# Queries ahead of scores in six slots, the first norm step behind the outputs, statistics in other slots, one value copy ahead, and one matmul for both parts of the reciprocals

## What is computed

```python
lat, ctx = layer_norm(layernorm(x)), layer_norm(context)
q = lat @ Wq;  k, v = split(ctx @ Wkv);  k = apply_rope(k, cos, sin)
attn = softmax(clip(q @ k.T * 64**-0.5, -11, 11))        # per batch and head
x = x + (attn @ v) @ Wo + bo                             # first layer
h = rmsnorm(layernorm(x)) * gamma1
q2 = h @ Wq + bq;  k2, v2 = split((h @ Wdown + bdown) @ Wup + bup)
att = softmax(q2 . k2 over the 8 of a group / sqrt(8))   # 16 x 16 per token
x1 = layernorm(x) + (att . v2) @ Wo + bo
h2 = rmsnorm(x1) * gamma2;  gate = softmax(h2 @ Wg + bg)
out = x + x1 + sum_e gate[e] * (h2 @ We[e])
```

## Time and profile before

| | us |
|---|---|
| median of 3 runs | 317.58 |
| the three runs | 317.51, 317.58, 318.62 |
| the profiled execution | 318.85 |
| its span (first to last instruction) | 317.0 |
| granted TensorE clock, mean | 0.996 |

### The profile page before, as it was taken

How to read it: one execution, slowest core, us unless ns; L and a number is a source line. 1 busy time by engine, 2 the same in 40 slices (tenths; PEclk the granted TensorE clock), 3 DMA queues, 4 the chain that set the end, 5 groups by cost and what they waited for, 6 DMA issues and landing times.

```text
span 317.0 us, 6676 instructions
## 1 busy us (share of the span) xinstructions
PE 295.0 (93%) x2514; PEld 206.9 (65%) x2514; DVE 241.6 (76%) x448; ACT 164.0 (52%) x326; POOL 208.6 (66%) x207
## 2 busy tenths in 40 slices
PE   6888999999999999998999999999999999899983
PEld 6776576666668766665777676566786665486651
DVE  2985997675884849899888788977647699687856
ACT  2446456667443735573425555874426468404741
POOL 5445875765572839786645777498927588868764
PEclk9999999999999999999999999999999999999998
DMA  7563412111210111111111112011101100000001
GB/s 207 169 160 90 134 44 68 52 35 46 58 26 9 38 31 35 36 33 33 35 35 33 28 27 50 13 40 37 32 19 33 47 7 2 0 19 0 3 0 33
DMA packets 16319, 14.24 MB, mean 45 GB/s; under 512 B 4832, under 2 KB 11808, under 8 KB 16288
## 3 DMA queue, kind: packets, MB, share of 16 engines
q1 hardware_dynamic: 14992, 13.49, 16.2%
q10 hardware_dynamic: 1296, 0.33, 0.5%
HBM read 4.89 MB, written 0.52 MB: 17 GB/s over the span
## 4 chain that ended last, share of the span: by engine, by line
PE 54%; DVE 20%; issue 7%; POOL 5%; ACT 5%; DMA 4%; SPq 3%; POOLq 0%; ACTq 0%; DVEq 0%
PE pv L631 12%; PE sc L617 10%; PE sums L652 7%; PE side L738 4%; PE pj_k L555 3%; SPq L522 3%; DVE ks L1262 3%; PE side L814 2%; PE pj_k L557 2%; PE pj_k L556 2%; DMA kswap<-ksin 2%; DMA sin_in<-in_L_xattn_sin_dram 2%; DVE ksin L1326 2%; ACT e L926 2%; POOL e L1768 1%
## 5 line engine op out<-in xcount | busy, mean ns | idle before, releaser
L1768 POOL TENSOR_SCALAR e<-e 128x1024 f32<-128x1024 f32 x64 | 71.6, 1118 | 64.2 <-ACT e L926 56.8
L926 ACT ACTIVATE e<-sc 128x1024 f32<-128x1024 f32 x64 | 65.6, 1025 | 31.3 <-PE sc L617 31.2
L617 PEld LDWEIGHTS sc<-qs,ks 64*128 64x128 f32 x768 | 49.6, 185 | 25.9 <-issue 24.0
L617 PE MATMUL sc<-qs,ks 64*128 64x256 f32 x768 | 62.5, 294 | 2.3 <-ACT e L926 2.2
L631 PE MATMUL pv<-e,v 128*64 128x256 f32 x512 | 62.3, 385 | 1.6 <-POOL e L1768 1.1
L1761 POOL TENSOR_TENSOR krot<-kcos,kswap 128x512 f32<-128x512 f32 x32 | 45.7, 1429 | 9.4 <-DMA kswap<-ksin 7.6
L631 PEld LDWEIGHTS pv<-e,v 128*64 128x64 f32 x512 | 34.1, 136 | 24.0 <-issue 6.8
L934 ACT ACTIVATE u<-pv 128x256 f32<-128x256 f32 x32 | 12.4, 386 | 61.6 <-PE pv L631 61.6
L1262 DVE TENSOR_TENSOR ks<-krot,ks 128x512 fp32r<-128x512 f32 x32 | 32.4, 1012 | 0.1
L1326 DVE TENSOR_TENSOR ksin<-pj_k,sinT 128x512 f32<-128x512 f32 x32 | 21.9, 685 | 3.8 <-PE pj_k L557 3.5
L918 ACT ACTIVATE v<-pj_k 128x512 f32<-128x512 f32 x28 | 16.5, 600 | 13.9 <-PE pj_k L557 13.5
(11 more groups left out here) (293 smaller groups left out, 578.1 us busy)
## 6 DMA issues: line engine op xcount, KB each, us to landing
kswap<-ksin SPq DMA_DIRECT2D x126, 64.0 KB, 2.0
ctx_in<-in_ctx_dram SPq DMA_DIRECT2D x4, 256.0 KB, 3.5
prod<-in_L_xattn_Wkv_dram SPq DMA_DIRECT2D x2, 512.0 KB, 6.3
x_in<-in_x_dram SPq DMA_DIRECT2D x1, 512.0 KB, 6.4
prod<-in_L_xattn_Wq_dram SPq DMA_DIRECT2D x1, 512.0 KB, 7.2
wo<-in_L_xattn_Wo_dram SPq DMA_DIRECT2D x1, 512.0 KB, 4.4
fwe<-in_L_ffn_We_dram SPq DMA_DIRECT2D x1, 512.0 KB, 4.4
out_dram<-x_in SPq DMA_DIRECT2D x3, 128.0 KB, 1.8
```

The source lines that it names most:

```text
L617: last = nc.tensor.matmul(sc[:, h, c * NT:(c + 1) * NT], ks[rows, j % 3, k_part, chunk], qs[rows, j % 2, q_part, :], start=(k_part + q_par ...
L926: nc.scalar.activation(e[:, j % 3, :, 2 * half:2 * half + 2, :].rearrange("p h c n -> p h (c n)"), sc[:, :, :], ACT.Exp, scale=SCALE).then ...
L1768: nc.gpsimd.tensor_scalar(a, a, EXP_HIGH, EXP_LOW, ALU.min, ALU.max).then_inc(s_clip, 1)
```

## The change

In slots where nothing stands on TensorE between the second half of the scores and the next keys but these keys (`queries_ahead`: 6, 9, 14, 17, 22, 25), the queries of the next pair are made ahead of `scores(slot, 0)`. Where the "a" step of a slot is `norm0` (`after_outputs`: 9, 17, 25), it stands behind `times_values` on TensorE, and its take behind `key_lo` on VectorE. `recS[:, 1]` becomes odd * rounded - rec: in even rows this is minus the reciprocal, rounded, in odd rows minus the rest. `spread` has -1 in an even and in the odd row next to it, so that one matmul adds both parts. It needs a second `affine_select` on GpSimd at the start and a small reduction in slot 0 for `odd`. The statistics of batches 2 and 3 go from slots 9 and 17 to slots 4 and 12 (batch 1 stays in slot 1). In slots 22 and 23 the first of two value copies goes ahead of the moe step.

```diff
--- before.py
+++ after.py
@@ -205,6 +205,18 @@
     return n < 4
 
 
+def queries_ahead(slot):
+
+    return 1 <= slot <= NPAIR - KEYS_AHEAD - 1 and not (side_step(slot - 1, "b") or side_step(slot - 1, "c")
+                                                       or value_units(slot - 1))
+
+
+def after_outputs(slot):
+
+    step = side_step(slot, "a")
+    return step is not None and step[0] == "norm0"
+
+
 def projections():
 
     units = []
@@ -311,7 +323,9 @@
 
 
         e_added = moe.rearrange("p t e d -> p (t e d)").rearrange("p (j c h n) -> p j c h n", j=2, c=2, h=2)
+
         recS = sb("recS", [128, 2, NT], fp32r)
+        odd = sb("odd", [128, 1])
 
         f_stat = sb("f_stat", [128, TT, 6])
         f_mv = sb("f_mv", [128, TT, 2])
@@ -721,8 +735,7 @@
                     for i in range(2):
                         p = 2 * int(name[4]) + i
                         dst = side[:, i * NT:(i + 1) * NT]
-                        nc.tensor.matmul(dst, spread[:, p, :], recS[:, 0, :], start=True, stop=False)
-                        last = nc.tensor.matmul(dst, spread[:, p, :], recS[:, 1, :], start=False, stop=True)
+                        last = nc.tensor.matmul(dst, spread[:, p, :], recS[:, 1, :], start=True, stop=True)
                 elif name == "out_proj":
                     if b == 0:
                         pe.wait_ge(ld["wo"], 16)
@@ -839,6 +852,8 @@
                 elif slot + 1 < NPAIR:
                     queries(slot + 1)
                 side_at(slot - 1, "c")
+                if queries_ahead(slot):
+                    queries(slot + 1)
                 if slot == 0:
                     keep_busy(WARM_UP["scores"], pv_bank)
                 if 0 <= slot < NPAIR:
@@ -846,13 +861,16 @@
 
                 if slot == 0:
                     keys(KEYS_AHEAD)
-                side_at(slot, "a")
-                if 0 <= slot + 1 < NPAIR and slot + KEYS_AHEAD < NPAIR:
+                if not after_outputs(slot):
+                    side_at(slot, "a")
+                if 0 <= slot + 1 < NPAIR and slot + KEYS_AHEAD < NPAIR and not queries_ahead(slot):
                     queries(slot + 1)
                 if 2 <= slot <= NPAIR and slot % 2 == 0:
                     sums(slot - 1)
                 if 1 <= slot <= NPAIR:
                     times_values(slot - 1)
+                if after_outputs(slot):
+                    side_at(slot, "a")
                 if slot == 0:
                     values(0)
                     values(1)
@@ -1135,9 +1153,15 @@
                 if 0 <= slot < NPAIR:
                     exps(slot, 1)
 
+                units = value_units(slot)
+                step = side_step(slot, "b")
+                if step and step[0].startswith("moe"):
+                    for n in units[:1]:
+                        value_copy(n)
+                    units = units[1:]
                 if slot < NPAIR - 3:
                     side_taken(slot, "b")
-                for n in value_units(slot):
+                for n in units:
                     value_copy(n)
                 if 0 <= slot + KV_AHEAD < NPAIR:
                     key_hi(slot + KV_AHEAD)
@@ -1345,7 +1369,9 @@
                 nc.vector.reciprocal(rec, sum_bank[:, 0:NT]).then_inc(s_rec, 1)
                 dve.wait_ge(s_rec, b + 1)
                 own(nc.vector.tensor_copy(recS[:, 0, :], rec))
-                split_lo(recS[:, 1, :], rec, recS[:, 0, :]).then_inc(s_recS, 1)
+
+                nc.vector.scalar_tensor_tensor(recS[:, 1, :], f(recS[:, 0, :]), odd[:, :], rec,
+                                               ALU.mult, ALU.subtract).then_inc(s_recS, 1)
 
 
             def tokens(b):
@@ -1676,7 +1702,10 @@
                 if slot == 0:
                     dve.wait_ge(s_const, 3)
                     nc.vector.tensor_copy(spread[:, :, :], spread_f[:, :, :]).then_inc(s_spread, 1)
-                side_taken(slot, "a")
+                    own(nc.vector.tensor_reduce(odd[:, :], ident.rearrange("p (a two) -> p two a", two=2)[:, 1, :],
+                                                AX, ALU.add))
+                if not after_outputs(slot):
+                    side_taken(slot, "a")
                 second_layer(slot, "early")
                 if 1 <= slot + 1 < NPAIR:
                     query_lo(slot + 1)
@@ -1684,13 +1713,19 @@
                     split_latT(b + 1)
                 if 1 <= slot + 1 < NPAIR:
                     key_lo(slot + 1)
+                if after_outputs(slot):
+                    side_taken(slot, "a")
                 second_layer(slot, "mid")
                 second_layer(slot, "late")
                 side_taken(slot, "b")
                 if more:
-                    if p == 1:
-                        ctx_statistics(b + 1)
-                        tokens_statistics(b + 1)
+
+                    if slot == 1:
+                        ctx_statistics(1)
+                        tokens_statistics(1)
+                    if p == 4 and b + 2 < NB:
+                        ctx_statistics(b + 2)
+                        tokens_statistics(b + 2)
                     if p == 2:
                         ctx_normalise(b + 1)
                         tokens_normalise(b + 1)
@@ -1744,7 +1779,10 @@
             nc.gpsimd.memset(sum_rows[:, 24:32], 1.0).then_inc(s_const, 1)
             own(nc.gpsimd.memset(spread_f[:, :, :], 0.0))
             sp_v = spread_f[:, :, :].rearrange("k (i q) (h c) -> k i q h c", q=2, h=2)
-            nc.gpsimd.affine_select(out=sp_v, in_=sp_v, compare_op=ALU.not_equal, fill=1.0, base=0,
+
+            own(nc.gpsimd.affine_select(out=sp_v, in_=sp_v, compare_op=ALU.not_equal, fill=-1.0, base=0,
+                                        pattern=[[-8, PAIRS // 2], [-64, 2], [-32, 2], [0, DH]], channel_multiplier=1))
+            nc.gpsimd.affine_select(out=sp_v, in_=sp_v, compare_op=ALU.not_equal, fill=-1.0, base=-1,
                                     pattern=[[-8, PAIRS // 2], [-64, 2], [-32, 2], [0, DH]], channel_multiplier=1)\
                 .then_inc(s_const, 1)
             ctx_rstd(0)
```

## The result

The changed kernel takes 314.12 us (median of 4 runs, 312.95 to 314.33) beside 317.54 for the kernel before on the same chip; the ratio is 0.9859 (95% interval 0.983 to 0.9888). The forecast was 312.6 in 310.8 to 315.3: faster, and inside the range. Measured once more, the changed kernel gave 313.19 beside 317.84, 0.9856 (0.984 to 0.9872).

What follows compares the result with a forecast made beforehand. The prediction took TensorE's stream as the bound in the loop over slots. Its terms, 1.73 + 0.2 + 1.28 + 0.66 + 1.0 + 0.1 = 5.0, taken from the median 317.58 gave 312.6 us, range 310.8 to 315.3.

Steps and rivals of the forecast that it cites:

- Slots 9 and 10, 17 and 18: Norm steps: 1.73 won in slots 9 and 10; 0.2 over slots 12 to 17, then 1.28 as in slot 10.
- the queries' place: Between scores and outputs: queries made ahead of the scores free their old place, 0.54 a slot, nothing in slot 6.
- Slots 12 to 16: Moved statistics make VectorE 1.66 late at first; some 1.1 is given back, 0.55 late at values(18) and slot 16.
- the bound of 1.66: Upper bound on VectorE's lateness at values(18) and slot 16 from slot 12's statistics; the lower bound was 0.
- Slots 22 to 24: One value copy ahead of moe frees the keys, moe1 waits for its bank: 0.66 won with slot 22's queries.
- Slots 25 to 31: Slots 25 and 26: norm1 at S+4.4 for S+4.7, plus 0.70 from the norm steps: 1.0 won.
- Start and tail: Start: ctx_rstd 0.35 late but covered, reduction for odd costs nothing; tail: 0.1 won, bounds 0 and 0.94.
- The cover of 1.1: At the start: slack left before ctx_rstd's reader at 7.86, so the second affine_select's delay would not count.
- Rival 3: Slots 9, 17, 25: norm0's take behind key_lo holds later scores; slower, 318.0 or 319.6; chance 0.05.
- Rival 2: TensorE gets nearly all its removed work and waits, 9.1 together: 308.5, likelier 310.5; chance 0.13.
- Rival 4: Parts work but off the path, as in slot 6; only 1.5 is won: 316.1; chance 0.07.
- Rival 1: VectorE bounds slots 12 to 17, the 1.66 is not given back: 314.2; chance 0.2.

Runs made afterwards that it cites:

- The statistics run twice: Changed kernel with VectorE taking slot 12's six statistics operations twice, 1.85 us more work: median 318.52 us.
- slot 27: Changed kernel with GpSimd's sum of the experts of the second half begun in slot 27, not slot 24: median 313.83 us.
- combined: Changed kernel with statistics one place earlier in slots 4 and 12 and GpSimd's second expert sum begun behind slot 26's first clip: 312.04 us, ratio 0.9835 to the kernel before.
- the first two experiments: Changed kernel with scores put back ahead of the queries, 314.16 us; changed kernel with reciprocals again repeated by two matmuls, 315.65 us.

## Why the prediction was right, point by point

**Slots 9 and 10, 17 and 18.** 1.74 for 1.73, 2.05 for 2.03. In slot 17 the step was right: naming VectorE's take as what is late next and timing it (norm1 waits 0.52 for it), and there the queries' place, norm0's and its second matmul are partly the same gain. In slot 9 the 0.01 is in part luck. The forecast had TensorE at norm1 at S + 4.1 and held by the take until S + 4.27. The single outputs step was mis-sized (1.03 for 0.9), so TensorE's own stream came there at S + 4.26: it filled just the wait that the forecast had there. In slots 22 and 25 the same step cost about 0.1 each of the 0.54.

**Slots 12 to 16.** The mechanism was right, the size not: VectorE was taken as 0.55 late at values(18), and TensorE waited 0.16. All in all 0.15 was lost here for 0.55. Counted from scores(13,1), VectorE was 1.75 late behind the statistics (forecast 1.66) and 0.17 late before slot 15 was over. It idled 0.91 as before, and the rest came back where the forecast said, in operations that no longer met GpSimd. The low part of latT, before and after:

```profile
129.28 1.22 DVE L1262 TENSOR_TENSOR latT<-latT_f,latT 128x256 fp32r<-128x256 f32 x1
...
127.49 0.43 DVE L1286 TENSOR_TENSOR latT<-latT_f,latT 128x256 fp32r<-128x256 f32 x1
```

That is 0.79. The rounding of latT gave 0.40 (0.68 to 0.28), less_maximum 0.27 and a split of the keys 0.13: 1.6 together, where 1.1 was forecast. This is the term that was mis-sized. The long split of the keys in slot 15 took 2.19 before and 2.20 after, so that meeting stayed. The statistics run twice show why the term was risky: the next 1.85 us cost 6.25 by slot 17. So the reckoning behind the bound of 1.66, that lateness is lost at most one for one, doesn't hold: neither a new meeting with GpSimd nor the clock was in it. The Trainium skill (SBUF — State Buffer, Who interferes with whom) has the former: of a VectorE operation with two SBUF inputs and a GpSimd operation that reads SBUF, the one that comes second is shut out until the other ends. The 2.65 of the split in that run, which ends 0.55 behind GpSimd's product (122.34 + 2.35), agrees.

**Slots 22 to 24.** 0.56 for 0.66. The keys' waits went, the expert step waits 0.58 at 196.48. The prediction gives the 0.66 without its terms, so only the total can be compared.

**Slots 25 to 31.** Wrong by 0.56, the largest miss. Norm1 was timed there by slot 9 and no other engine looked at. The changed kernel's GpSimd:

```profile
214.49 2.95 POOL L1868 TENSOR_TENSOR moe<-moe 128x512 f32<-128x512 f32 x3
...
217.93 1.30 POOL L1799 TENSOR_TENSOR krot<-kcos,kswap 128x512 f32<-128x512 f32 x1
219.19 0.75 POOL L1885 TENSOR_TENSOR x_in<-x_in,bo_r 128x256 f32<-128x256 f32 x1
220.02 2.16 POOL L1806 TENSOR_SCALAR e<-e 128x1024 f32<-128x1024 f32 x2
```

It works without a gap from the expert sum to the second clip, which ends at 222.18, and the sums start at 222.24. TensorE came 0.6 earlier and found it busy: 0.83 had been won by scores(26,0), and 0.45 of it was gone at scores(26,1). With the expert sum out of the way that wait is gone in two kernels (slot 27, and combined), which shows the cause.

**Start and tail.** c_rstd comes 0.29 later (5.27, 4.98; forecast 0.35). The cover of 1.1 that the prediction read off was no property of the kernel: it was the late transfer of `sin_in`. In this execution `ctx_n` starts at 6.68, 0.04 behind c_rstd and 0.74 behind the copy of `cos_in` where it otherwise comes 0.55 behind (7.31 to 7.86). So it was held by an estimated 0.2, a term that the prediction put at nothing. In the tail the four repeats are 0.94 shorter on TensorE and nothing of it arrives, as forecast: 0.47 of it is now the wait for `on` (L751). The sign of the last 0.1 was wrong. The row split by scalar_tensor_tensor takes 0.48 for the 0.42 of the plain subtraction; in the tail VectorE has no gap from it to the takes, and they come 0.06 late.

**The rivals.** Rival 3 is out at the size that made it slower: the take ends at S + 4.2 in slot 9 and the scores of slots 10, 18 and 26 don't wait. Of its kind is only norm1's wait of 0.52 in slot 17. Rival 2 is out by the first two experiments: neither the queries nor the removed matmuls count everywhere. Rival 4 holds for slot 6 only. Rival 1 priced 1.6; 0.15 was lost in slots 13 to 16, and putting the statistics back gave 0.51 there.

**The total.** In the loop and tail 4.5 was won of 5.0. It is that near because 0.4 less was lost in slots 13 to 16 than forecast, which covers most of the 0.56 that failed to come in slots 25 to 31. The two profiled executions lie 5.9 apart and the medians of their runs 3.4, because that of before was 1.3 above its median and that of after the fastest of its four; the start alone differs by 1.3. What made the other three runs of after 1.0 to 1.4 longer no kept trace shows. The second pair of medians gives 4.65.

## What to carry to other kernels

When a wait is removed on the engine that bounds, time the next event on each of the other engines, GpSimd's light duties too, and count the gain only up to it: slots 17 and 18 came out to 0.02 that way, slots 25 and 26, where one engine was left out, at half. Where two engines arrive within 0.1 us of each other, as in slot 9, only an experiment tells which one holds. Put moved work into an idle gap, ahead of the instruction behind it and not after. Read gains of a few tenths from marks inside the loop, since the start moves by more. A cover that rests on when a transfer lands is not one to count on.

## What the runs showed of the hardware

Behind a wait of 2.33 us TensorE's granted clock fell to 0.5 (1.2 of 2.4 GHz) for a few us. The slow matmuls cost 1.53 us, and 2.97 where a second wait of 1.59 followed the first, each on top of the waits. In the changed kernel the longest wait between 20 and 262 us is 0.84, in the kernel before it is 1.1, and the clock stays at 1.00 in both. With matmuls that nobody reads in the place of the waits it stayed at 1.00 too. The Trainium skill (TensorE: Matmul & The Clock Gate, Part 1) has a gate between these two levels that follows how busy TensorE is; the windows agree, with 1.00 before and 0.50 behind the two waits.

A VectorE operation with two SBUF inputs lost 1.97 us to one GpSimd operation (0.68 to 2.65), and TensorE's scores waited for its result: a delay of 1.85 us on VectorE became 3.5 before the clock came into it.
